# A tanh recurrence in 64 parallel chunks before a quantised FFN: warm-up steps replaced by guess steps among the x products and by corrected first steps

## The chip, the cores and the metric

One core of a Trainium2 chip. The metric is the device time of one execution in microseconds; lower is better.

## The reference

x is (2, 2048, 512) in float32, the start state (2, 512). The part of the reference that matters here:

```python
xW = einsum('ntd,dh->nth', x, Wx) + b
def step(prev_h, xw_t):
    next_h = tanh(xw_t + prev_h @ Wh)
    return next_h, next_h
_, hs = scan(step, h0, swapaxes(xW, 0, 1))       # 2048 steps, one after the other
h = relu(quant_linear(hs, w1, b1))                # 512 -> 2048
out = x + quant_linear(h, w2, b2)                 # 2048 -> 512
```

quant_linear quantises its input to 0..255 with one scale from the maximum over the whole tensor, its weights to -128..127 with one scale per row, and its bias by the product of the scales. So the first scale needs every state, and the second every hidden value.

## The kernel before, in words

**Chunks.** The 2048 steps of both sequences are cut into 64 chunks of STEPS = 32. All run at once: a state is a tile of 512 features (KT = 4 tiles of 128 partitions) by COLS = 128 columns (64 chunks x 2 sequences, chunk by chunk). Each chunk needs the last state of the chunk before it. That state is found by a warm-up: WARM = 36 steps over the columns 0 to 125 (SEAM = 126), each column running through the chunk ahead of the one whose start it gives. The recurrence forgets its start, so that warm-up and true state meet.

**Stages on PE** (`block.tensor`):
1. x products (`xw_group`, L459): 8 groups of 512 tokens, per group 4 output tiles of 4 float32 matmuls (two records each in the trace). ACT evacuates each tile with the bias to `xw` (L731). w1 and w2 land beside them and DVE makes integers of them (`integers`, L912 to L934). After each of the first three groups 16 transposes (L445) turn four blocks of w1, and ACT stores them.
2. Warm-up: three opening steps and 18 coarse guess steps with Wh and state in float16 (`products`, L484 and L491, with the x product added by a matmul with a scaled identity, L501), then 14 split steps of 48 float16 matmuls (`split_step`, L527): high and low part of Wh and of the state.
3. Main pass (`main_pass`, L484 and L491): 32 steps of 16 float32 matmuls. DVE adds the x product into the bank (`add_xw`, L953), ACT writes tanh of it as the next state (`exact_step`, L767), DVE takes each state's maximum (L1022). Inside a step, k = 0 and 1 of all four output tiles come first, then k = 2 and 3 tile by tile, so that the first tile's add and tanh run behind the others' matmuls.
4. Check of the seams (`check_seams`): DVE takes the largest difference between each chunk's last state and the start state used for the next chunk, PE turns and spreads it with the maximum (L563, L568). If it is above SEAM_TOL = 2^-17, every engine enters the repair loop (`while_seams_differ`), which puts the last states in as start states and runs the main pass again. Meanwhile PE turns 16 more weight blocks (`turn_middle`) and ACT stores them.
5. First FFN product of 8 groups (L639) with maxima over it, a short stage for the second scale (with idle products, L429), then the second FFN product (L679) with stores.

**What orders the work.** Nothing is scheduled by a program: each engine's instructions run as written, with counting semaphores. `state_ready` counts tanh tiles, `z_ready` PE's finished sums, `sum_ready` DVE's adds, `xw_free` evacuated x tiles, `w_stored` stored weight blocks.

**Where things lie.** One large SBUF tile, `arena`, holds nearly everything, and PSUM is the tensor `bank` of 8 banks; in the trace most operations are `bank<-arena` or `arena<-bank`, so lines tell them apart.

The order inside a main step on PE:

```python
for k in range(2):
    pe.wait_ge(state_ready, (n - 1) * KT + k + 1)
    for j in range(KT):
        matmul(bank[:, par * KT + j, lo:hi], weights[:, k, j * P:(j + 1) * P], source(k), ...)
for j in range(KT):
    for k in range(2, KT):
        ...
    mm.then_inc(z_ready, 1)
```

## Time and profile before

| | |
|---|---|
| Time, median of 3 runs | 540.9 us (539.24 to 541.88) |
| Span of the profiled execution | 538.5 us |
| Busy, share of the span | PE 98%, PE weight loads 62%, DVE 64%, ACT 47%, POOL 10% |
| Moved by DMA | 61.13 MB |

The span goes from the first to the last instruction of one execution on the profiler; its own time as a run is not among the three, which lie 0.7 to 3.4 us above the span. A line such as L459 is a line of the kernel before. A record's duration holds the time until its result is written, so neighbouring matmuls overlap in the view and the spacing of their starts is what a queue of them costs.

### The profile page before, as it was taken

The numbers are of one execution on the slowest core, as the hardware profiler recorded it, in microseconds if no ns is written. First come the engines' busy times: TensorE is split into PE (matmuls) and PEld (weight loads), VectorE is DVE, ScalarE is ACT, GpSimd is POOL, SyncE is SP. The second block draws the span as 40 slices with busy tenths as digits, with TensorE's granted clock in tenths as the row PEclk, the third lists the DMA queues.
The fourth block names the chain that finished last, engine by engine and source line by source line (L and its number), as shares of the span: only waits on it lengthen the run. The fifth ranks groups of instructions, "written<-read, shape, count | busy, mean of one in ns | idle before, by whom it ended". The sixth has DMA issues, their size and how long they took to land.

```text
span 538.5 us, 11182 instructions
## 1 busy us (share of the span) xinstructions
PE 525.4 (98%) x3527; PEld 332.4 (62%) x3546; DVE 342.4 (64%) x695; ACT 251.3 (47%) x558; POOL 56.0 (10%) x42
## 2 busy tenths in 40 slices
PE   7999999999999999999999899999999899999997
PEld 2444444449999999999999544444444444444443
DVE  0888880004377654555455798888868667778875
ACT  1323222226655432233223755655553866666662
POOL 2000000000000000000000000000000315354445
PEclk9999999999999999999999999999999899999999
DMA  8986500000000000000000077710000248888884
GB/s 289 323 326 252 220 1 0 0 1 1 0 0 0 2 0 0 0 0 0 0 0 0 4 292 302 301 41 0 1 1 2 78 147 311 282 318 283 319 299 145
DMA packets 21138, 61.13 MB, mean 114 GB/s; under 512 B 2032, under 2 KB 2176, under 8 KB 17536
## 3 DMA queue, kind: packets, MB, share of 16 engines
q1 hardware_dynamic: 20448, 59.84, 30.4%
q10 hardware_dynamic: 576, 1.05, 0.5%
q8 instruction: 9, 0.15, 0.1%
q0 software_dynamic: 96, 0.01, 0.1%
q14 instruction: 9, 0.07, 0.0%
HBM read 39.93 MB, written 20.97 MB: 113 GB/s over the span
## 4 chain that ended last, share of the span: by engine, by line
PE 94%; DVE 1%; DMA 1%; ACT 1%; issue 1%; DVEq 0%; ACTq 0%
PE bank L639 20%; PE bank L459 20%; PE bank L679 20%; PE bank L491 12%; PE bank L484 12%; PE bank L527 7%; DMA arena<-x_t 1%; PE bank L501 1%; PE bank L445 1%; PE bank L429 1%; ACT w1t L749 0%; DVE arena L1188 0%; ACT w2t L752 0%; DVE acc_max L1148 0%; DVE arena L1208 0%
## 5 line engine op out<-in xcount | busy, mean ns | idle before, releaser
L767 ACT ACTIVATE arena<-bank 128x126 f16<-128x126 f32 (+3 forms) x324 | 72.8, 281 | 104.1 <-DVE bank L953 74.7
L459 PE MATMUL bank<-arena 128*128 128x512 f32 (+1 forms) x256 | 111.8, 597 | 1.7 <-DMA arena<-x_t 1.7
L639 PE MATMUL bank<-arena,w1t 128*128 128x512 bf16 (+1 forms) x502 | 110.2, 379 | 2.1 <-DVE arena L1117 1.6
L679 PE MATMUL bank<-arena,w2t 128*128 128x512 bf16 x504 | 111.0, 379 | 0.6 <-DVE arena L1212 0.2
L414 POOL TENSOR_SCALAR arena<-arena,bq 128x512 f32<-128x512 f32 x32 | 52.7, 1661 | 470.0 <-DVEq L1233 415.1
L639 PEld LDWEIGHTS bank<-arena,w1t 128*128 128x128 bf16 x512 | 49.9, 98 | 62.2 <-issue 1.6
L679 PEld LDWEIGHTS bank<-arena,w2t 128*128 128x128 bf16 x512 | 49.1, 98 | 62.6 <-DVE arena L1212 4.5
L459 PEld LDWEIGHTS bank<-arena 128*128 128x128 f32 x256 | 48.5, 191 | 62.8 <-issue 61.8
L1148 DVE TENSOR_REDUCE acc_max<-arena 128x2 f32<-128x1024 f32 x60 | 71.6, 1217 | 15.8 <-ACT arena L844 15.2
L491 PE MATMUL bank<-arena 128*128 (+2 forms) x680 | 75.5, 261 | 0.5 <-ACT arena L742 0.5
L844 ACT COPY arena<-bank 128x1024 f32<-128x1024 f32 x56 | 56.7, 1012 | 40.4 <-PE bank L639 40.4
L484 PE MATMUL bank<-arena 128*128 (+2 forms) x680 | 75.1, 261 | 0.0
L868 ACT ACTIVATE arena<-arena,bias,scale 128x512 uint16 (+1 forms) x93 | 69.9, 807 | 10.5 <-DVE arena L1200 10.0
L953 DVE TENSOR_TENSOR bank<-bank,arena 128x128 f32<-128x128 f32 x128 | 38.4, 300 | 56.0 <-PE bank L491 42.3
L491 PEld LDWEIGHTS bank<-arena 128*128 128x128 f32 (+1 forms) x680 | 70.0, 169 | 0.8 <-ACT arena L742 0.7
L484 PEld LDWEIGHTS bank<-arena 128*128 128x128 f32 (+1 forms) x680 | 69.6, 169 | 0.6 <-issue 0.6
L731 ACT ACTIVATE arena<-bank,b_sb 128x512 f32<-128x512 f32 (+1 forms) x32 | 22.0, 687 | 80.5 <-PE bank L459 80.4
L1200 DVE TENSOR_SCALAR arena<-arena 128x512 bf16<-128x512 uint16 x96 | 33.2, 359 | 21.4 <-PE bank L679 18.5
L982 DVE TENSOR_SCALAR arena<-arena 128x504 f16 (+1 forms) x21 | 8.8, 422 | 55.1 <-ACT arena L731 41.0
L527 PE MATMUL bank<-arena 128*128 128x126 f16 x672 | 37.2, 218 | 0.0
L527 PEld LDWEIGHTS bank<-arena 128*128 128x128 f16 x672 | 37.0, 98 | 0.3 <-ACT arena L767 0.2
L912 DVE TENSOR_REDUCE w_absmax<-arena 128x2048 f32 x8 | 18.3, 2286 | 15.8 <-DMA arena<-w 11.8
(87 smaller groups left out, 260.6 us busy)
## 6 DMA issues: line engine op xcount, KB each, us to landing
spill<-arena SPq DMA_DIRECT2D x12, 1024.0 KB, 3.9
arena<-spill SPq DMA_DIRECT2D x12, 1024.0 KB, 8.4
arena<-w SPq DMA_DIRECT2D x8, 1024.0 KB, 5.9
arena<-x_t SPq DMA_DIRECT2D x32, 256.0 KB, 4.0
y_t<-arena SPq DMA_DIRECT2D x32, 256.0 KB, 2.1
arena<-x_t SPq DMA_DIRECT2D x7, 1024.0 KB, 8.2
arena<-x_t ACTq DMA_DIRECT2D x4, 256.0 KB, 6.2
arena<-wx SPq DMA_DIRECT2D x4, 256.0 KB, 5.5
```

The source lines that it names most:

```text
L414: nc.gpsimd.tensor_scalar(xb[:, d], xb[:, d], bq2[:, d:d + 1], None, ALU.add).then_inc(xb_ready, 1)
L459: mm = nc.tensor.matmul(bank[:, j, :], wx_sb[:, k, j * P:(j + 1) * P], x_in[:, g, k, :], start=(k == 0), stop=(k == KT - 1))
L484: nc.tensor.matmul(bank[:, par * KT + j, lo:hi], weights[:, k, j * P:(j + 1) * P], source(k), start=(first and k == 0), stop=False)
L491: mm = nc.tensor.matmul(bank[:, par * KT + j, lo:hi], weights[:, k, j * P:(j + 1) * P], source(k), start=False, stop=(k == KT - 1 and then ...
L527: return nc.tensor.matmul(bank[:, par * KT + j, 0:SEAM], weights[:, k, j * P:(j + 1) * P], state[:, 1 - par, k, 0:SEAM], **ends)
L639: mm = nc.tensor.matmul(bank[:, f % 8, :], w1t[:, k, f * P:(f + 1) * P], q[:, slot, k, :], start=(k == 0), stop=(k == KT - 1))
L679: return nc.tensor.matmul(bank[:, 4 + d, :], w2t[:, f, d * P:(d + 1) * P], hq[:, f % HQ_RING, :], start=(f == 0), stop=(f == FT - 1))
L767: return nc.scalar.activation(dst, bank[:, par * KT + j, lo:hi], ACT.Tanh, scale=scale)
L844: nc.scalar.copy(keep[:, at, f:f + 2, :], bank[:, f % 8:f % 8 + 2, :]).then_inc(acc_kept, 1)
L868: nc.scalar.activation(u[:, f % U_RING, :], src, ACT.Relu, bias=bias1[:, f:f + 1], scale=scale1[:, f:f + 1]).then_inc(u_ready, 1)
L953: nc.vector.tensor_tensor(z, z, xw[:, slot, j, 0:cols], ALU.add).then_inc(sum_ready, 1)
L1148: nc.vector.tensor_reduce(acc_max[:, g, f:f + 2], source, AX_X, ALU.max).then_inc(seen, 1)
```

## The change

The warm-up stage is gone. In its place:

- **Guess steps among the x products** (`guess_step`). Groups of x are computed in the order 3, 4, 5, 6, 7, 0, 1, 2 (X_ORDER), in 32 units of one output tile (four matmuls). From unit 13 on, the guess step for slot 13 to 31 of the chunk is put between k = 1 and k = 2 of the unit with the same number: 16 float16 matmuls with 126 columns. The first guess is tanh of slot 12's x product. ACT writes 256 times the x product into the bank before (`lay_guess`), and PE adds onto it; four matmuls with zeros (`bits_set`) make the banks add. The last guess step gives the start states of the main pass, after 19 steps.
- **Main pass** as before, but from less exact start states; in the first 12 steps DVE writes the sum before tanh to `fixed` in SBUF instead of back to the bank.
- **Correction** (`fix_step`, `fix_tanh`, `lay_fixed`, `fixes`). Twelve more steps after it: the error of a slot (new state less old, float16) times Wh in float16 is added to the saved sum before tanh, which gives the new state of the next slot, whose error goes into the next step. Slots 13 to 32 keep their states. The repair flag is raised if the last error is above 2^-17, or the first one times 2^-11 is, or Wh is too large for float16.
- The first x group now goes k by k through all four banks. The three lots of w1 transposes stand behind units 4, 7 and 10. DVE makes the float16 Wh after the fourth integer block, in two passes instead of four, with a maximum of Wh. Tokens are numbered on by `tokens(g)`, so that the corrected groups are quantised from `fixed`.

```diff
-PRE = 4
-WARM = PRE + STEPS
-COARSE = 22
+GUESS = 20
+FIXED = 12
+LEFT_OUT = 2.0 ** -11
+FIRST_GROUP = (STEPS - GUESS) // SLOTS_PER_GROUP
+X_ORDER = tuple((i + FIRST_GROUP) % GROUPS for i in range(GROUPS))
+TURN_BEHIND = {4: 0, 7: 1, 10: 2}
-MIDDLE_BANKS = (2, 3, 4, 5, 6, 7)
+MIDDLE_BANKS = (4, 5, 6, 7, 2, 3)
...
+            def guess_step(s):
+                n = s - (STEPS - GUESS)
+                pe.wait_ge(guess_laid, n)
+                for j in range(KT):
+                    for k in range(KT):
+                        if j == 0 and k % 2 == 0:
+                            pe.wait_ge(guess_ready, 2 * (n - 1) + k // 2 + 1)
+                        mm = nc.tensor.matmul(guess_bank(s, j), wh_high[:, k, j * P:(j + 1) * P],
+                                              guess[:, (n - 1) % 2, k, 0:SEAM], start=False,
+                                              stop=(k == KT - 1), skip_group_check=True)
+                    if j % 2 == 1:
+                        mm.then_inc(guess_z, 1)
...
+            def fix_step(t):
+                at, par = 4 * (t % 2), (t - 1) % 2
...
+                pe.wait_ge(fixed_laid, t)
+                pe.wait_ge(error_ready, 2 * t - 1)
+                for j, k in ((0, 0), (1, 0), (0, 1), (1, 1), (2, 0), (3, 0)):
+                    add(j, k)
+                pe.wait_ge(error_ready, 2 * t)
+                for j, k in ((0, 2), (0, 3), (1, 2), (1, 3)):
+                    mm = add(j, k)
+                mm.then_inc(fixed_z, 1)
+                for j, k in ((2, 1), (2, 2), (2, 3), (3, 1), (3, 2), (3, 3)):
+                    mm = add(j, k)
+                mm.then_inc(fixed_z, 1)
...
+                    for k in range(KT):
+                        mm = x_product(i, j, k)
...
+                        if k == 1 and unit > STEPS - GUESS:
+                            if unit == STEPS - GUESS + 1:
+                                pe.wait_ge(wh_split, 1)
+                            guess_step(unit)
...
-            first_guess_step()
...
-            with pe.Fori(COARSE // 2, WARM // 2) as half:
-                split_step(half * 2, 0)
-                split_step(half * 2 + 1, 1)
             pe.wait_ge(wh_in, 16)
             pe.wait_ge(h0_in, 16)
-            main_pass(WARM)
+            pe.wait_ge(xw_free, KT + GROUPS * KT)
+            main_pass(0)
+            for t in range(1, FIXED + 1):
+                fix_step(t)
...
+            def fix_tanh(t):
+                at = 4 * (t % 2)
+                for a in range(2):
+                    act.wait_ge(fixed_z, 2 * (t - 1) + a + 1)
+                    nc.scalar.activation(fixed[:, t - 1, 2 * a:2 * a + 2, :],
+                                         bank[:, at + 2 * a:at + 2 * a + 2, 0:COLS], ACT.Tanh,
+                                         scale=1.0 / WH_SCALE).then_inc(fixed_ready, 1)
...
+            for t in range(1, FIXED + 1):
+                fix_tanh(t)
+                if t + 2 <= FIXED:
+                    lay_fixed(t + 2)
...
+            def fix_pair(t, a):
+                dve.wait_ge(fixed_ready, 2 * (t - 1) + a + 1)
+                nc.vector.tensor_tensor(error[:, t % 2, 2 * a:2 * a + 2, 0:SEAM],
+                                        fixed[:, t - 1, 2 * a:2 * a + 2, BATCH:COLS],
+                                        states[:, t, 2 * a:2 * a + 2, BATCH:COLS],
+                                        ALU.subtract).then_inc(error_ready, 1)
```

How the change moves the instructions, at three places. First PE, at the end of the x products (L459 before). Before, the loop over the last four groups was followed by the opening of the warm-up (L484 and L491 with Wh, L501 with the identity):

```order
L473 COMPARE_AND_BRANCH
L484 MATMUL bank<-arena 128x124 x8
L491 MATMUL bank<-arena 128x124 x2
L501 MATMUL bank<-arena,idf 128x124
L491 MATMUL bank<-arena 128x124 x2
L501 MATMUL bank<-arena,idf 128x124
```

Now (L468 an x product, L553 the zeros, L483 a guess step) the x products go on in fours with a guess step between each two fours:

```order
L464 MATMUL bank<-id,w1t 128x128 x16
L468 MATMUL bank<-arena 128x512 x6
L553 MATMUL bank<-arena 128x256 x4
L468 MATMUL bank<-arena 128x512 x4
L483 MATMUL bank<-arena 128x126 x16
L468 MATMUL bank<-arena 128x512 x4
L483 MATMUL bank<-arena 128x126 x16
```

Each four are the second half of one unit and the first half of the next; the last guess step is followed by two x products and then by the main loop.

Second, PE at the end of the main pass. Before, its loop was followed at once by the turning of weights (L445) and the spreading of the maximum (L563, L568):

```order
L553 COMPARE_AND_BRANCH
L445 MATMUL bank<-id,w1t 128x128 x16
L445 MATMUL bank<-id,w2t 128x128 x28
L563 MATMUL bank<-id,stat 1x128 x2
L445 MATMUL bank<-id,w2t 128x128 x8
```

Now 192 matmuls, 16 for each correction step, stand between the loop and the same row:

```order
L505 COMPARE_AND_BRANCH
L515 MATMUL bank<-arena 128x126 x192
L464 MATMUL bank<-id,w1t 128x128 x16
L464 MATMUL bank<-id,w2t 128x128 x28
L574 MATMUL bank<-id,stat 1x128 x2
L464 MATMUL bank<-id,w2t 128x128 x8
```

Third, ACT at the same place. Before, the loop over the main steps (L767) was followed by the stores of turned weights:

```order
L767 ACTIVATE arena<-bank 128x128
L809 REGISTER_ALU
L809 COMPARE_AND_BRANCH
L749 COPY w1t<-bank 128x4x128 x4
L752 COPY w2t<-bank 128x512 x12
```

Now the last two main steps (L797) are written out, with the laying of saved sums (L817) between them, and then each correction step's two tanh (L824) are followed by the laying for the step after the next:

```order
L797 ACTIVATE arena<-bank 128x128 x4
L817 ACTIVATE bank<-arena 128x4x128
L797 ACTIVATE arena<-bank 128x128 x4
L817 ACTIVATE bank<-arena 128x4x128
L824 ACTIVATE arena<-bank 128x256 x2
L817 ACTIVATE bank<-arena 128x4x128
L824 ACTIVATE arena<-bank 128x256 x2
```

The pattern goes on to the twelfth step; the stores of turned weights come after it.

## Rows read from the trace of the kernel before

**Rows 1.** The page: PE's busy time (part 1) and granted clock by slice (part 2).
```profile
PE 525.4 (98%) x3527; PEld 332.4 (62%) x3546; DVE 342.4 (64%) x695; ACT 251.3 (47%) x558; POOL 56.0 (10%) x42
...
PEclk9999999999999999999999999999999899999999
```

**Rows 2.** Busy time by stage: split steps, main steps, the stage behind them.
```profile
core 0: us, PE busy (x) PEld busy (x) DVE busy (x) ACT busy (x) POOL busy (x), PEclk, DMA share, GB/s
...
146.00:183.00 37.00, 37.00 (x672) 36.93 (x673) 28.02 (x111) 20.71 (x113) 0.00 (x0) 1.00 0.00 0
183.00:297.40 114.40, 114.40 (x1028) 114.40 (x1026) 58.50 (x160) 35.48 (x129) 0.00 (x0) 1.00 0.00 0
297.40:305.40 8.00, 5.84 (x70) 4.20 (x71) 5.95 (x20) 7.67 (x18) 0.00 (x0) 1.00 0.01 2
```

**Rows 3.** Order of time on PE, x products: start, us, instruction [idle before it].
```profile
5.03 2.75 PE L459 MATMUL bank<-arena 128*128 128x512 f32 x4 [0.35 <-DMA arena<-x_t]
9.14 12.26 PE L459 MATMUL bank<-arena 128*128 128x512 f32 x28 [1.36 <-DMA arena<-x_t]
...
22.12 13.95 PE L459 MATMUL bank<-arena 128*128 128x512 f32 x32
35.91 1.06 PE L445 MATMUL bank<-id,w1t 128*128 128x128 bf16 x16
...
51.49 68.89 PE L459 MATMUL bank<-arena 128*128 128x512 f32 x160
120.21 0.60 PE L484 MATMUL bank<-arena 128*128 128x124 f16 x8
```

**Rows 4.** Order of time: a weight load of PE, and DVE's integer blocks.
```profile
6.34 0.61 PEld L459 LDWEIGHTS bank<-arena 128*128 128x128 f32 x2 [0.84 <-DMA arena<-wx]
...
12.91 2.29 DVE L912 TENSOR_REDUCE w_absmax<-arena 128x2048 f32 x1 [11.77 <-DMA arena<-w]
...
18.93 1.23 DVE L934 TENSOR_SCALAR w1t<-arena 128x2048 f32 x1 [0.15 <-DVE arena L924]
...
42.28 1.23 DVE L934 TENSOR_SCALAR w1t<-arena 128x2048 f32 x1 [0.15 <-DVE arena L924]
```

**Rows 5.** Order of time on PE: the split steps and the first main matmuls.
```profile
145.94 37.25 PE L527 MATMUL bank<-arena 128*128 128x126 f16 x672
183.02 2.02 PE L484 MATMUL bank<-arena 128*128 x16
```

**Rows 6.** Groups by line and shape: busy us, mean ns of one, idle before.
```profile
L953 DVE TENSOR_TENSOR bank<-bank,arena 128x128 f32<-128x128 f32 x128 | 38.4, 300 | 56.0 <-PE bank L491 42.3
L527 PE MATMUL bank<-arena 128*128 128x126 f16 x672 | 37.2, 218 | 0.0
...
L767 ACT ACTIVATE arena<-bank 128x128 f32 x128 | 35.5, 277 | 79.1 <-DVE bank L953 74.7
...
L1022 DVE TENSOR_REDUCE slot_max<-arena x32 | 21.9, 686 | 0.0
...
L1034 DVE TENSOR_TENSOR arena<-arena 128x378 f32<-128x378 f32 x1 | 0.5, 543 | 0.0
```

**Rows 7.** Order of time: handovers at the warm-up's start and in a main step.
```profile
120.41 0.69 ACT L731 ACTIVATE arena<-bank,b_sb 128x512 f32<-128x512 f32 x1 [2.55 <-PE bank L459]
...
121.35 0.42 PE L491 MATMUL bank<-arena 128*128 128x124 f16 x2 [0.54 <-ACT arena L742]
...
185.63 1.64 DVE L953 TENSOR_TENSOR bank<-bank,arena 128x128 f32<-128x128 f32 x4 [2.11 <-PE bank L491]
186.08 0.69 ACT L767 ACTIVATE arena<-bank 128x128 f32 x2 [2.26 <-DVE bank L953]
```

**Rows 8.** Busy time by stage, two us each, before the second FFN product.
```profile
415.00:417.00 2.00, 1.30 (x10) 0.48 (x7) 1.50 (x2) 1.01 (x1) 0.00 (x0) 1.00 0.00 0
417.00:419.00 2.00, 0.68 (x9) 0.32 (x7) 1.43 (x6) 1.50 (x2) 0.00 (x0) 1.00 0.91 260
...
421.00:423.00 2.00, 2.00 (x6) 0.68 (x5) 1.02 (x5) 2.00 (x4) 0.00 (x0) 0.50 0.00 0
```

More of the change, by code:

```diff
@@ L95 @@
 STAT_LINKS = 6
+STAT_FIRST = 4
 def rnn_ffn_program(nc, xT, h0T, wx, wh, bT, w1, b1T, w2, b2T, ident, yT):
@@ L481, in products @@
+            def products(n, at, state):
                 for k in range(2):
-                    pe.wait_ge(state_ready, (n - 1) * KT + k + 1)
+                    pe.wait_ge(state_ready, n * KT + k + 1)
                     for j in range(KT):
-                        nc.tensor.matmul(bank[:, par * KT + j, lo:hi],
-                                         weights[:, k, j * P:(j + 1) * P], source(k),
-                                         start=(first and k == 0), stop=False)
+                        nc.tensor.matmul(bank[:, at + j, 0:COLS], wh_sb[:, k, j * P:(j + 1) * P],
+                                         state(k), start=(k == 0), stop=False)
@@ L489, in products @@
                         if j == 0:
-                            pe.wait_ge(state_ready, (n - 1) * KT + k + 1)
-                        mm = nc.tensor.matmul(bank[:, par * KT + j, lo:hi],
-                                              weights[:, k, j * P:(j + 1) * P], source(k),
-                                              start=False,
-                                              stop=(k == KT - 1 and then_add is None))
-                    if then_add is not None:
-                        mm = then_add(j)
@@ L550, in split_step @@
+                            pe.wait_ge(state_ready, n * KT + k + 1)
+                        mm = nc.tensor.matmul(bank[:, at + j, 0:COLS],
+                                              wh_sb[:, k, j * P:(j + 1) * P], state(k),
+                                              start=False, stop=(k == KT - 1))
                     mm.then_inc(z_ready, 1)
@@ L797, in _, with guess_pair @@
[L797 to L809 removed]
+            def guess_pair(s, a):
+                at = 4 + 2 * (s % 2) + a
+                return bank[:, at, 0:2 * COLS].rearrange("p (k c) -> p k c", k=2)[:, :, 0:SEAM]
@@ L820, in repair @@
             def repair(r):
-                main_pass(WARM + r * STEPS)
+                early_steps(r * STEPS)
+                with act.Fori(FIXED // 2, STEPS // 2) as half:
+                    for par in range(2):
+                        late_step(r * STEPS, half * 2 + par, par)
                 act.wait_ge(flag_ready, r + 1)
```

484 lines of the change are left out of this document (245 added, 239 removed).

## The prediction

> **What bounds the kernel now.** I read the page's shares and slices first: PE is busy 98% of a 538.5 us span, at the full clock but for one slice [rows 1]. The sum is made against that span; the three timed runs have their median, 540.9 us, 2.4 us above it, and I carry the difference in us over to the median. A high PE share does not say that every matmul is limited by the array, so the second view was busy time by stage [rows 2]: in the split warm-up PE is busy 37.00 of 37.00 us, in the main steps 114.40 of 114.40, and only in the eight microseconds after them do holes appear (5.84 of 8.00). DVE and ACT have slack in each of these stages. So until 297.4 us the time is the number of matmuls times the spacing at which PE starts them, and a change there is worth what it takes off PE's queue, if the other engines still keep up. The third view, PE's order of time, gives the spacings [rows 3, 5].
>
> **What is removed.** The whole warm-up goes: from the first guess matmul at 120.21 us [rows 3] to the first main matmul at 183.02 us [rows 5], **62.8 us**. Of this the 14 split steps are 37.1 us (672 matmuls), the 21 coarse ones the rest. POOL's copy of the identity goes too, beside other work, and so does DVE's second half of the split of Wh: it ran while PE worked on x products, so it is worth nothing.
>
> **What is added between the x products.** 19 guess steps of 16 matmuls, 128x126 f16. The row of the same form gives 672 starts in 37.25 us, whose last record alone lasts 0.218 [rows 5, 6]: (37.25 - 0.16) / 672 = 55.2 ns. So 304 x 55.2 ns = **+16.8 us**, all on PE's path, since PE has no idle time there. A change from x products to 128-column matmuls and back costs something: 32 records between two lots of transposes take 35.91 - 22.12 = 13.79 us, while the last 160 take 120.21 - 51.49 = 68.72, or 13.74 per 32 [rows 3]. That is 0.05 us a time, 19 times: **+1.0**. Four idle matmuls of 256 columns: **+0.4** (twice 55 ns each).
> The Trainium skill, TensorE: Matmul & The Clock Gate, section Back-to-back issue gap, speaks against this part: pairs of weight load and matmul sustain about 81 ns at 128 columns. By that figure the 304 would be an estimated 24.6 us instead of 16.8; the trace disagrees, its 672 such pairs stand at 55 ns.
>
> Is a guess step ever late? A unit of x products (four matmuls, eight records) is 3.4 us, with the guess step in its middle 4.3 us. From one step's sums to the next step ACT must do two tanh of 2x126 columns, lay x products of a later step into a bank (504 columns) and evacuate 512: about 0.4 + 0.4 + 0.7 + 0.7 = 2.2 us, the last from the 0.69 of such an evacuation [rows 7]. It fits twice into 4.3, and the tanh comes first. So no PE wait is charged. DVE now splits Wh after the fourth integer block, which ends at 43.5 us [rows 4]; two passes of the size of 1.23 end by about 46, and the first guess step comes at about 54. The four w2 blocks are then some 5 us later, with 60 us of x products over them.
>
> **The opening.** Before, bank 0 took all its four k before bank 1 began, so PE sat until x's later quarters landed at 9.14, with four records done since 5.03 [rows 3]. Now all four banks take k=0, then k=1. k=1's weights are there at 6.34 [rows 4], and 16 records at 0.43 us (68.72 / 160) reach from 5.03 to 11.9, past 9.14. 32 records end at 5.03 + 13.75 = 18.8 instead of 21.2: **-2.4 us**. The next unit needs the second group of x, queued right behind the first w block, which landed at 12.91 [rows 4]; its 1 MB should follow in some 3 us, before 18.8. The transposes now stand one unit later, at about 22.2, and their integers are ready at 20.16 [rows 4]. If the DMA comes later the gain is nil: bounds 0 and -2.5.
>
> **A new stop before the main steps.** They wait for the last evacuation of x. PE's last x record ended at 120.38, and ACT evacuated from 120.41 for 0.69, to 121.10 (PE's next start that needed ACT, 121.35, came after a tanh more) [rows 7]. With a handover of 0.06, between the two named below, PE could go on at 121.16; without the wait it would at 120.21. **+0.95**. The main steps themselves stay 32 x 16 matmuls with add and tanh behind them. The first 12 write their sums to SBUF instead of PSUM; ACT starts 0.15 us after DVE's end (185.63 + 0.30, then 186.08) [rows 6, 7] and both idle over a microsecond per step, so nothing is charged.
>
> **The correction steps.** Twelve steps that nothing covers: PE, ACT and DVE wait for each other in a ring. The engines' queues per step: PE 16 matmuls, ACT two tanh of 256 columns and one laying of 512, DVE two differences of 252 and a maximum over 512. Prices: tanh 256 lies between 277 ns (128 columns) [rows 6] and 0.69 us (512) [rows 7], by columns 0.41; a difference of 252 lies between 300 ns (128) and 543 (378) [rows 6], 0.42. The ring through the second half: ten matmuls till its sums are there, 9 x 0.055 + 0.218 = 0.71; tanh 0.41; difference 0.42; three handovers, of which rows show 0.03 (PE to ACT, 120.38 to 120.41) and 0.15 (DVE to ACT) [rows 7], say 0.2 together: **1.75 us a step**. ACT's own work, 0.41 + 0.41 + 0.69 = 1.5, and DVE's, 0.42 + 0.42 + 0.69 = 1.5, fit below it, though not by much. Lower bound 1.5 (those queues, no handovers), upper 2.2 (0.15 for each handover, and the laying or the maximum in the way of the next tanh or difference).
> Lead-in after the last main matmul: add 0.30 and tanh 0.28 with handovers, 0.9; DVE has the maximum of step 31 (686 ns [rows 6]) in front of the first difference; two differences; 1.8 us. Then 11 rings and the last ten-odd matmuls, 0.78: 1.8 + 19.3 + 0.8 = **+21.8 us**.
>
> **Behind it** stand the 16 transposes and their stores, the seam's maximum, the scale and the quantising, as before. The seam's chain loses one difference and the add, and has more in one piece; PE was waiting for ACT's stores as much as for it. Taken as **-0.3**, bounds -1 and +1. The FFN stages keep their matmuls; the order of token groups and the one new wait of ACT (for DVE's third quantising, which DVE does before the first maxima) are costed at nothing: DVE runs two groups ahead of PE there.
>
> Sum: -62.8 + 16.8 + 1.0 + 0.4 - 2.4 + 0.95 + 21.8 - 0.3 = -24.5 us. Span 538.5 - 24.5 = 514.0; **time 540.9 - 24.5 = 516.4 us**. With the bounds (ring 1.6 to 1.95, opening, tail) this case reaches from 513 to 520.5.
>
> **The rivals.**
> Long rings (14%). Handovers sit three times in each step, and ACT's laying comes right before the next tanh. At 2.25 us a step the stage is 12 x 0.5 = 6 us longer: 522.4. Against it: the queues sum to 1.5 us only.
> The clock falls (13%). In the correction steps PE streams 16 x 0.055 = 0.88 us of each 1.75, about half. For it: before the FFN's second half, PE was busy 1.30 and then 0.68 of 2 us, and by 421 us the granted clock was 0.50, the 1.2 GHz level [rows 8]. Against it: through the 8 us after the main steps, where some 68 matmuls of 128 columns stream 3.8 us (47%), it stayed at 1.00 [rows 2], and half is nearer to that. At 1.2 GHz 128 columns take 0.107 us instead of 0.053, ten in a row 0.5 more: 12 x 0.55 = 6.6, and about 1.5 more until the first FFN products have it back: 524.5.
> The Trainium skill, TensorE: Matmul & The Clock Gate, section A second HAM failure mode: psum-queue depth-cycling, states this rule: frequent short idling of PE between groups of matmuls makes the clock swing between its levels. By it the result is that of this rival.
> The repair loop runs (4%): the one that ends slower. The flag is raised when a difference left after 12 corrected steps is above 2^-17 = 7.6e-6, or the first one times 2^-11 is. Carrying out the new arithmetic on the reference's inputs, with float16 where the kernel has it, I get 0.0010 for the first difference (0.06 of its limit) and 4.9e-6 for the last (0.64 of it), shrinking by some 0.64 a step. It decides from a start error 1.6 times as large. Then a main pass of 114.4 us is run again [rows 2], with a seam check of about 8 and a copy of some 4: 516.4 + 126 = 643 us.
> The interleaving isn't free (3%): if PE's queue loses 0.4 us at each of 19 steps, by late tanh or late weights, 7.6 us: 524.
>
> **Chances.** The sum as it stands has 66%; 516.4 is its value. All cases but the repair loop are faster by far more than 0.5% (2.7 us, about what a measurement of this kernel can tell from no change): faster 0.95, same 0.01 for something unseen that eats all of it, slower 0.04. The range takes in the forecast's own and three of the rivals, 511.5 to 525 us.
>
> **What the profile would show.** Right: no hole in PE from 5 us to the end of the x products, at about 136.0 us; the first record of the main steps about 0.9 us after that; 12 groups of correction matmuls 1.7 to 1.9 us apart with PE idle less than a microsecond in each; the first FFN product near 281 us; PEclk 9 in all slices but one. Wrong: idle time of the guess matmuls "from ACT" (the interleaving), correction tanh ending over 2 us apart (the ring), a PEclk digit below 9 near 260 us (the clock), or more than 512 main products (the repair).

## The result, and the profile after

| | before | after |
|---|---|---|
| Time, median of 4 runs each | 540.71 us | **517.88 us** (517.40 to 518.74) |
| Ratio, 95% interval | | 0.9585 (0.9568 to 0.9602) |
| Span of the profiled execution | 538.5 us | 515.9 us (its run: 517.75 us) |

The change takes 22.6 us off the span, where the sum said 24.5. The page after, busy time and granted clock by slice, beside [rows 1]:

```profile
PE 496.1 (96%) x2954; PEld 300.8 (58%) x2954; DVE 310.6 (60%) x587; ACT 256.5 (50%) x455; POOL 55.8 (11%) x41
...
PE   8999999999999999999857999999998999999997
...
PEclk9999999999999999999999999999998999999999
```

PE runs 573 matmul records fewer (3527 in [rows 1]). The slices "857" are the correction steps and what follows them, the new stretch in which PE waits for the other engines. Stage by stage, PE's order of time (start, us, instruction, idle before it), beside [rows 3, 5]:

```profile
4.87 18.47 PE L468 MATMUL bank<-arena 128*128 128x512 f32 x40 [0.20 <-DMA arena<-wx]
23.18 1.06 PE L464 MATMUL bank<-id,w1t 128*128 128x128 bf16 x16
...
55.65 1.04 PE L483 MATMUL bank<-arena 128*128 128x126 f16 x16
56.53 3.65 PE L468 MATMUL bank<-arena 128*128 128x512 f32 x8
60.02 1.04 PE L483 MATMUL bank<-arena 128*128 128x126 f16 x16
...
135.19 1.94 PE L468 MATMUL bank<-arena 128*128 128x512 f32 x4
138.33 2.05 PE L493 MATMUL bank<-arena 128*128 x16 [1.21 <-ACT arena L729]
...
255.48 1.04 PE L515 MATMUL bank<-arena 128*128 128x126 f16 x16 [1.50 <-ACT bank L817]
257.21 1.04 PE L515 MATMUL bank<-arena 128*128 128x126 f16 x16 [0.69 <-DVE arena L1037]
259.06 1.04 PE L515 MATMUL bank<-arena 128*128 128x126 f16 x16 [0.81 <-DVE arena L1037]
...
275.51 1.06 PE L464 MATMUL bank<-id,w1t 128*128 128x128 bf16 x16
...
282.64 7.54 PE L637 MATMUL bank<-arena,w1t 128*128 128x512 bf16 x33 [1.21 <-DVE arena L1167]
```

The last x record ends at 135.19 + 1.94 = 137.13 and lasts 0.60 (the others of the group are done before), so it starts at 136.53, and the x products leave PE's queue one spacing of 0.43 later, at 136.96. Put against the sum, stage by stage:

| stage | forecast, us | measured, us |
|---|---|---|
| end of x products (before 120.21) | +15.8 (16.8 + 1.0 + 0.4 - 2.4) | +16.75 |
| stop before the main steps | 0.95 | 1.37 (136.96 to 138.33) |
| main steps, 114.4 before | 114.4 | 115.48 (138.33 to 253.81) |
| correction steps | 21.8 | 21.70 (253.81 to 275.51) |
| from there to the first FFN product, 7.97 before | 7.67 | 7.13 |
| the rest | +0 | +0.17 |

The x products, the stop and the main steps miss upward by 0.95 + 0.4 + 1.1, some 2.5 us; the tail and the correction steps give 0.6 back, the rest takes 0.2, and some 2 us remain, 24.5 against 22.6. The experiments take the larger ones one by one.

### The profile page after: what moved, and what is told of

It reads as the page before. It is cut to its first block, busy times and chain, and to the rows that moved or that the text cites. A ratio compares the mean times of both kernels' runs of the same rounds, so it can differ in the third digit from the quotient of the medians.

```text
span 515.9 us, 9080 instructions
## 1 busy us (share of the span) xinstructions
PE 496.1 (96%) x2954; PEld 300.8 (58%) x2954; DVE 310.6 (60%) x587; ACT 256.5 (50%) x455; POOL 55.8 (11%) x41
## 3 DMA queue, kind: packets, MB, share of 16 engines
q10 hardware_dynamic: 576, 1.05, 0.6%
## 4 chain that ended last, share of the span: by engine, by line
PE 93%; DVE 3%; ACT 2%; issue 1%; DVEq 0%
PE bank L468 22%; PE bank L637 22%; PE bank L677 21%; PE bank L493 11%; PE bank L499 11%; PE bank L483 3%; PE bank L515 2%; PE bank L448 1%; DVE arena L1037 1%; PE bank L464 1%; ACT arena L824 1%; ACT w1t L737 0%; DVE arena L1238 0%; DVE arena L1262 0%; DVE acc_max L1198 0%
## 5 line engine op out<-in xcount | busy, mean ns | idle before, releaser
L468 PE MATMUL bank<-arena 128*128 128x512 f32 x256 | 116.2, 602 | 0.2 <-DMA arena<-wx 0.2
L1198 DVE TENSOR_REDUCE acc_max<-arena 128x2 f32<-128x1024 f32 x60 | 71.6, 1217 | 15.8 <-ACT arena L875 15.2
L468 PEld LDWEIGHTS bank<-arena 128*128 128x128 f32 x256 | 47.3, 192 | 51.4 <-issue 50.3
L994 DVE TENSOR_TENSOR arena<-bank,arena 128x128 f32 x48 | 14.0, 292 | 91.5 <-PE bank L499 91.2
L493 PE MATMUL bank<-arena 128*128 x512 | 63.5, 277 | 1.2 <-ACT arena L729 1.2
L499 PE MATMUL bank<-arena 128*128 x512 | 62.4, 275 | 0.0
L493 PEld LDWEIGHTS bank<-arena 128*128 128x128 f32 x512 | 59.7, 192 | 2.2 <-issue 2.0
L499 PEld LDWEIGHTS bank<-arena 128*128 128x128 f32 x512 | 59.7, 192 | 0.0
L797 ACT ACTIVATE arena<-bank 128x128 f32 (+1 forms) x80 | 22.2, 277 | 48.6 <-DVE bank L1001 46.1
L1001 DVE TENSOR_TENSOR bank<-bank,arena 128x128 f32<-128x128 f32 x80 | 24.0, 300 | 36.5 <-PE bank L499 27.6
L1250 DVE TENSOR_SCALAR arena<-arena 128x512 bf16<-128x512 uint16 x96 | 31.4, 340 | 20.7 <-PE bank L677 17.7
L729 ACT ACTIVATE arena<-bank,b_sb 128x512 f32<-128x512 f32 x32 | 21.7, 687 | 34.9 <-PE bank L468 34.9
L797 ACT ACTIVATE arena<-arena x48 | 14.8, 309 | 30.7 <-DVE arena L994 26.6
L762 ACT ACTIVATE arena<-bank 128x252 f16<-128x252 f32 x36 | 13.7, 380 | 27.5 <-PE bank L483 26.4
```

The costliest lines, as they stand in the source:

```text
L468: return nc.tensor.matmul(bank[:, j, :], wx_sb[:, k, j * P:(j + 1) * P], x_in[:, X_ORDER[i], k, :], start=(k == 0), stop=(k == KT - 1))
L493: nc.tensor.matmul(bank[:, at + j, 0:COLS], wh_sb[:, k, j * P:(j + 1) * P], state(k), start=(k == 0), stop=False)
L499: mm = nc.tensor.matmul(bank[:, at + j, 0:COLS], wh_sb[:, k, j * P:(j + 1) * P], state(k), start=False, stop=(k == KT - 1))
L797: nc.scalar.activation(dst(j), src(j), ACT.Tanh).then_inc(state_ready, 1)
L1001: nc.vector.tensor_tensor(z, z, xw[:, s, j, :], ALU.add).then_inc(sum_ready, 1)
L1198: nc.vector.tensor_reduce(acc_max[:, g, f:f + 2], source, AX_X, ALU.max).then_inc(seen, 1)
```

## The experiments

### The stop before the main steps

PE's chain there, from the chain of waits (start, us, what):

```profile
137.16 0.70 ACT arena L729
137.86 0.47 issue
```

The wait ends with ACT's evacuation at 137.86, and then 0.47 us pass in which nothing is shown before the loop's first matmul. The forecast had 0.06 for this handover. The experiment puts the wait into the loop, where it is needed first (the second step uses the banks of the last x unit):

```diff
...
                     for par in range(2):
+                        if par == 1:
+                            pe.wait_ge(xw_free, KT + GROUPS * KT)
                         products(first + s + par, 4 - 4 * par, ...)
...
-            pe.wait_ge(xw_free, KT + GROUPS * KT)
+            pe.wait_ge(state_ready, KT)
             main_pass(0)
```

> The wait for the last evacuation of x stands before the second main step (whose banks it guards) instead of before the first; before the first stands only the wait for the four start-state tiles. In the trace of the changed kernel PE stood 1.42 us between the x products and the main steps, of which 0.69 are the evacuation and 0.48 its handover to PE. Theory A (the stop is nothing but that wait): the main steps begin within 0.1 us of the last x product's slot, time 517.9 - 1.4 = 516.5 us. Theory B (entering the loop on PE costs its 0.5 us whatever it waits for): 0.9 us off, about 517.0. Theory C (the evacuation is late for the second step as well): unchanged.

Measured: 516.66 us (514.96 to 516.93), 0.9554 (0.9535 to 0.9572), 1.2 us under the changed kernel's 517.88. PE no longer stops:

```profile
134.63 1.94 PE L468 MATMUL bank<-arena 128*128 128x512 f32 x4
136.40 1.95 PE L493 MATMUL bank<-arena 128*128 x16
...
253.43 1.04 PE L517 MATMUL bank<-arena 128*128 128x126 f16 x16 [1.50 <-ACT bank L819]
255.16 1.84 PE L517 MATMUL bank<-arena 128*128 128x126 f16 x16 [0.69 <-DVE arena L1039]
257.39 1.58 PE L517 MATMUL bank<-arena 128*128 128x126 f16 x16 [0.39 <-DVE arena L1039]
259.62 1.04 PE L517 MATMUL bank<-arena 128*128 128x126 f16 x16 [0.65 <-DVE arena L1039]
```

The last x record leaves the queue at 134.63 + 1.94 - 0.60 + 0.43 = 136.40, and the main steps start at 136.40. So the whole stop of 1.37 us is avoidable, its 0.47 us too: the loop is entered before anything is waited for. The first correction matmul comes 2.05 us earlier (253.43 instead of 255.48), of which 0.56 are not the edit's: in this execution the x products were that much earlier (134.63 instead of 135.19), for a reason given under the opening. And the span fell by only 1.0, since time is lost again behind that: the second and third group of correction matmuls take 1.84 and 1.58 instead of 1.04. The windows of two stretches (PE, PEld, DVE, ACT, POOL busy, then granted clock):

```profile
255.00:257.00 2.00, 1.84 (x16) 1.61 (x16) 1.71 (x5) 0.91 (x2) 0.00 (x0) 0.54 0.05 8
259.00:261.00 2.00, 1.04 (x16) 0.90 (x16) 1.61 (x4) 1.63 (x5) 0.00 (x0) 1.00 0.00 0
```

The granted clock is 0.54 here (0.61 in the two microseconds that follow), at its 1.2 GHz level for most of this stretch, and back at 1.00 by 259 us, in the middle of the same rings. This is the rival of the falling clock, but with two rings of 2.23 us instead of 1.85 and 1.73, so 0.9 us where it had 8.

### The slower first main steps

PE's main steps are 3.57 us apart from the fourteenth on, as before, but the first 13 are 3.66 us apart. The order of time in one that writes its sums to SBUF: the add of its first tile, the four tanh, and PE's next step in its two halves (k = 0 and 1, then k = 2 and 3); then the first half of the fourteenth step:

```profile
148.35 0.29 DVE L994 TENSOR_TENSOR arena<-bank,arena 128x128 f32 x1 [2.02 <-PE bank L499]
...
148.88 1.57 ACT L797 ACTIVATE arena<-arena  x4 [2.08 <-DVE arena L994]
149.35 2.04 PE L493 MATMUL bank<-arena 128*128 x16
151.22 1.95 PE L499 MATMUL bank<-arena 128*128 x16
...
185.91 1.95 PE L493 MATMUL bank<-arena 128*128 x16
```

and the group of these tanh over the whole run (busy us, mean ns of one, idle before):

```profile
L797 ACT ACTIVATE arena<-arena x48 | 14.8, 309 | 30.7 <-DVE arena L994 26.6
```

The tanh takes 309 ns from SBUF against 277 from PSUM [rows 6], and it starts 0.24 us after the add's end (148.35 + 0.29, then 148.88) against 0.15 [rows 7]. That is some 0.1 us for each tile, and it counts for one tile only, the first. Its tanh ends at 148.88 + 0.31 = 149.19, just ahead of the next step's first matmul at 149.35, and the half that begins there takes 2.04 (to its last result) where the fourteenth step's takes 1.95: that is the 0.09 by which the step is longer. The last tile's tanh ends at 148.88 + 1.57 = 150.45, and the half that reads it starts at 151.22 without a hole. Twelve steps write to SBUF and hold back the twelve steps behind them; the first step is long as well (3.70), and stays so with the sums in PSUM (3.67 in the run that follows), so that is not theirs. The experiment leaves the sum in PSUM, lets ACT read it there as before, and copies four sums at once behind the step's tanh:

```diff
-                        exact_tanh(first + s + par, lambda j: fixed[:, s + par, j, :],
+                        exact_tanh(first + s + par, lambda j: bank[:, 4 - 4 * par + j, 0:COLS],
...
+                    z = bank[:, at + j, 0:COLS]
...
-                    nc.vector.tensor_tensor(fixed[:, s, j, :], bank[:, at + j, 0:COLS], xw[:, s, j, :],
-                                            ALU.add).then_inc(sum_ready, 1)
+                    nc.vector.tensor_tensor(z, z, xw[:, s, j, :], ALU.add).then_inc(sum_ready, 1)
+                dve.wait_ge(state_ready, (n + 1) * KT + KT)
+                nc.vector.tensor_copy(fixed[:, s], bank[:, at:at + KT, 0:COLS]).then_inc(sum_kept, 1)
```

> In the first 12 main steps DVE adds into the bank, as in the others, ACT reads the bank, and DVE copies the four sums to SBUF afterwards, outside the chain. In the changed kernel these steps took 3.66 us each instead of 3.57. Theory A (the sum's way over SBUF makes the next step's first matmul late: handover 0.24 instead of 0.15, tanh 309 instead of 277 ns): back to 3.57, 1.0 us less, 516.9. Theory B (something else at the start of the main steps, such as the approximate start states or DVE's loop without the maximum): stays at 3.66, unchanged or more, since DVE has the copies too.

Measured: 517.34 us (516.17 to 518.78), 0.9575 (0.9555 to 0.9596). In the trace, against the same rows of the changed kernel (138.33 and 255.48, 117.15 apart), main start and first correction matmul are 116.11 apart:

```profile
137.59 2.05 PE L494 MATMUL bank<-arena 128*128 x16 [1.21 <-ACT arena L730]
...
253.70 1.04 PE L516 MATMUL bank<-arena 128*128 128x126 f16 x16 [1.50 <-ACT bank L818]
```

The 1.04 us, twelve times 0.09, are there in the trace. The times alone, 0.5 us apart with overlapping intervals, would not show it.

### The opening

The first x group goes bank by bank again:

```diff
...
-                    for to in range(KT):
-                        pe.wait_ge(xw_free, to + 1)
-                        mm = x_product(0, to, j)
...
+                    for k in range(KT):
+                        if j == 0:
+                            pe.wait_ge(wx_in[k], 16)
+                            pe.wait_ge(x0_in[k], 16)
+                        mm = x_product(0, j, k)
...
```

> Only the opening undone: the first x group goes bank by bank again, so PE waits in bank 0 for the later quarters of x. The prediction put the opening at 2.4 us; by the trace of the changed kernel it brought about 1.5, since PE's first records there stand 0.86 us apart instead of 0.43. Theory A (those first records are slow whatever follows, and the waits of before hid that): 1.5 us more, 519.4. Theory B (prediction): 2.4 more, 520.3.

Measured: 519.83 us (518.46 to 520.65), 0.9619 (0.96 to 0.9639): the median is 1.95 us above the changed kernel's, between the two theories' 1.5 and 2.4. PE's order of time:

```profile
8.55 15.93 PE L468 MATMUL bank<-arena 128*128 128x512 f32 x36 [1.22 <-DMA arena<-x_t]
24.31 1.06 PE L464 MATMUL bank<-id,w1t 128*128 128x128 bf16 x16
```

40 records are done at 24.31 against 23.18: 1.13 us between these two executions. Before, the fifth record began at 9.14 [rows 3], so 40 would have been done at 9.14 + 36 x 0.4295 = 24.6, and the change gained 1.4 against that. The 2.4 us of the forecast are not reached in this execution because the first records are slow. PE's weight loads in the changed kernel, each ahead of its record:

```profile
5.85 0.34 PEld L468 LDWEIGHTS bank<-arena 128*128 128x128 f32 x1 [0.52 <-issue]
6.71 0.34 PEld L468 LDWEIGHTS bank<-arena 128*128 128x128 f32 x1 [0.52 <-issue]
7.30 0.19 PEld L468 LDWEIGHTS bank<-arena 128*128 128x128 f32 x1 [0.25 <-issue]
```

They stand 0.86 us apart, then 0.59, and 0.43 from there on. The 40 records take 18.31 us where 40 x 0.4295 is 17.18. So 1.13 us go to the first records, which run at half the rate, as at the 1.2 GHz level. The windows of 4.8 to 7.3 us read a granted clock of 1.00 all the same, but the trace's first record of the clock begins at 7.02 us in this execution, so nothing stands under that figure.

How many records are slow differs from execution to execution. In the profile of a kernel that opens in the same way (the one with filled holes, below) all but the first stand 0.43 apart:

```profile
4.84 17.41 PE L468 MATMUL bank<-arena 128*128 128x512 f32 x40 [0.17 <-issue]
```

Over the twelve profiles of kernels with the new order the 40 records are done between 21.88 and 23.25 us, at 22.8 on average, and in each the full rate comes with the first record of the clock, from 4.38 to 7.37 us. With the old order PE waits for x in any case: 24.31 here, 24.6 before. So the order is worth 1.1 to 2.7 us, some 1.7 on average, and the forecast's 2.4 where the clock is up early. The same spread, 1.4 us, moves everything behind the opening, and it is why the experiments are compared by distances within a trace.

### What sets the ring

The changed kernel's first ring, from 255.48 on PE to 257.21; the order of time on ACT and DVE in it:

```profile
256.22 0.71 ACT L824 ACTIVATE arena<-bank 128x256 f32<-128x256 f32 x2 [0.86 <-PE bank L515]
...
256.64 0.75 DVE L1037 TENSOR_TENSOR arena<-arena 128x252 f16<-128x252 f32 x2
```

Ten matmuls to their sums 0.74; tanh 0.38; 0.04 to DVE; difference 0.42; 0.15 to PE: 1.73 us through the first half, where the forecast had 0.71 + 0.41 + 0.42 + 0.2 = 1.74. It had named this the ring through the second half; whether the two halves differ, the first of three experiments asks, by four matmuls in the first group instead of six, so that the first half's sums come two matmuls earlier (the two go to the last group):

```diff
-                for j, k in ((0, 0), (1, 0), (0, 1), (1, 1), (2, 0), (3, 0)):
+                for j, k in ((0, 0), (1, 0), (0, 1), (1, 1)):
...
```

> In each correction step PE issues four matmuls before it waits for the second difference instead of six, so the first sums are complete after 8 matmuls instead of 10. Theory A (the ring runs through the first half: ten matmuls, first tanh, first difference): each ring 0.11 us shorter, 1.73 to about 1.62, time 1.2 us less, 516.7. Theory B (the second difference, which ends some 0.18 us after a ring's first matmul, is then what the ring runs through): 1.73 to 1.68, 0.6 us less. If DVE's or ACT's queue set the pace: no change.

Measured: 518.23 us (516.69 to 519.03), 0.9587 (0.9568 to 0.9607). From the fourth ring on they are not shorter but longer, 1.77 us. The second group:

```profile
257.08 1.18 PE L515 MATMUL bank<-arena 128*128 128x126 f16 x16 [0.58 <-DVE arena L1037]
```

The group takes 1.18 instead of 1.04, so PE now stands inside it: the second difference comes about 0.33 us after the first, just what six matmuls take (6 x 0.055). With four ahead PE waits for it, and then twelve matmuls, not ten, lead to the second half's sums. Without those two the ring through the second half would be some 0.1 us shorter, an estimated 1.66, so the two halves lie within a tenth of a microsecond of each other, and neither theory came true.

Is DVE's queue in the way? Here the maxima over the corrected slots 1 to 11 are left out (one small copy, once, stands for them):

```diff
-                    nc.vector.tensor_reduce(slot_max[:, t:t + 1], fixed[:, t - 1, :, :], AX_XY, ALU.max)
...
+                        nc.vector.tensor_copy(slot_max[:, 1:FIXED], slot_max[:, FIXED + 1:2 * FIXED])
```

> Leaves out DVE's maxima of 512 columns over the corrected slots 1 to 11, so the input's scale lacks them. Theory A (the ring is 10 matmuls, tanh, difference and handovers; DVE has 0.4 us to spare per step): rings stay at 1.73 us, only the second one, which held two maxima, falls from 1.85 to 1.73; time 0.1 us less. Theory B (DVE's queue sets the pace): rings 0.3 or more shorter, 3 to 4 us less.

Measured: 518.09 us (one run). The rings stay at 1.73. Only the second one, 1.85 in the changed kernel where two maxima stand in it, becomes 1.73 too:

```profile
257.25 1.04 PE L515 MATMUL bank<-arena 128*128 128x126 f16 x16 [0.69 <-DVE arena L1037]
258.98 1.04 PE L515 MATMUL bank<-arena 128*128 128x126 f16 x16 [0.69 <-DVE arena L1037]
```

Is ACT's? The laying of a saved sum is done twice, and in a further kernel four times:

```diff
+                for i in range(2 - 1):
+                    nc.scalar.activation(bank[:, at:at + KT, 0:COLS], fixed[:, t - 1], ACT.Identity,
+                                         scale=WH_SCALE).then_inc(lay_link, 1)
+                    act.wait_ge(lay_link, (2 - 1) * (t - 1) + i + 1)
```

> ACT lays each saved sum twice, one after the other, so 0.6 us and a short wait more per correction step in ACT's queue. Theory A (ACT has 0.5 us between the end of a laying and the next tanh): rings longer by 0.2 us only, time 2 us more. Theory B (the ring is ACT's queue): 0.7 us a ring, 7 to 8 us more.

> The same with four layings: rings of about 3.5 us, in which PE has 0.88 us of matmuls, a quarter instead of half. This tests the rival on the clock. Theory A (clock held at half, but not at a quarter, as in the stage before the second FFN product): the granted clock falls to 0.50 within the correction steps, matmuls start every 0.107 us there, and time is 18 us more for ACT's queue plus 2 us or so until the FFN has the clock back. Theory B (the clock holds also at a quarter): 1.00 throughout, 18 us more.

Measured: 516.98 us with two (one run), rings of 1.84; 533.43 us with four (one run), rings of 3.105. The first time is below the changed kernel's although its rings are longer, by 1.05 us from the first correction matmul to the last: its mean granted clock is 1.00, so the clock never fell, and it says nothing on the layings. Twice, order of time on PE; four times, on ACT and on PE:

```profile
258.70 1.04 PE L516 MATMUL bank<-arena 128*128 128x126 f16 x16 [0.86 <-DVE arena L1042]
260.54 1.04 PE L516 MATMUL bank<-arena 128*128 128x126 f16 x16 [0.80 <-DVE arena L1042]
```

```profile
257.81 1.87 ACT L819 ACTIVATE bank<-arena 128x512 f32<-128x512 f32 x3
259.71 0.60 ACT L822 ACTIVATE bank<-arena 128x512 f32<-128x512 f32 x1
260.25 0.64 ACT L829 ACTIVATE arena<-bank 128x256 f32<-128x256 f32 x2
```

```profile
261.21 1.84 PE L516 MATMUL bank<-arena 128*128 128x126 f16 x16 [2.06 <-DVE arena L1042]
```

ACT's starts say what its queue costs: 260.92 - 260.25 = 0.67 for the two tanh, 1.90 / 3 = 0.63 for a laying ahead of another one, 0.54 for the last (259.71 to 260.25). That makes 0.67 + 0.63 + 0.54 = 1.84 with two layings and 0.67 + 1.90 + 0.54 = 3.11 with four, which are the rings measured, and 0.67 + 0.54 = 1.21 in the changed kernel: 0.5 us of slack in 1.73. So the ring is set by the latencies through PE, ACT and DVE, and by no engine's queue, except with the layings added. The long-rings rival is out. What was expected of the longer queues was too high, since durations were added where starts count.

With four layings the clock falls and stays down through this stage, as theory A had it: granted 0.63 from 259 to 262 us, 0.50 from there to 290, PE's groups of 1.84 instead of 1.04. The 533.43 us hold hardly any of that, since ACT's queue covers it.

### How far the repair loop is

Two kernels tighten the bound, by 0.6 and by 0.2, and change nothing else:

```diff
-SEAM_TOL = 2.0 ** -17
+SEAM_TOL = 0.6 * 2.0 ** -17
```

> The same kernel with the seam tolerance at 0.6 of its value. The arithmetic worked through for the prediction gave 0.64 of the limit for the last difference, so the flag should be raised once: a second main pass with its check, priced at 126 us: about 644 us. If the chip's difference is smaller than that arithmetic's, no repair and 517.9.

> The seam tolerance at 0.2 of its value, since 0.6 raised no flag. Theory A (the chip's last difference is near the arithmetic worked through for the prediction, if below 0.6 of the limit): the flag is raised and one repair runs, priced at 126 us (a main pass of 114.4, a seam check, a copy): about 644 us. Theory B (the chip's differences are much smaller than worked out): 517.9.

Measured: 517.39 us with 0.6 (one run), no repair; the last difference on the chip is below 0.6 of the bound, where I had worked out 0.64. With 0.2: **730.45 us** (one run), one repair. That is 212.6 us more than the changed kernel, where the rival had 126. The order of time on DVE and PE, and the window behind the second main pass:

```profile
481.29 0.88 DVE L1157 TENSOR_SCALAR arena<-arena,s_in_inv 128x512 uint16<-128x512 f32 x2 [71.06 <-issue]
495.36 19.82 PE L637 MATMUL bank<-arena,w1t 128*128 128x512 bf16 x81 [85.52 <-issue]
```

```profile
410.00:495.00 85.00, 0.00 (x0) 0.05 (x2) 7.42 (x20) 0.00 (x0) 0.00 (x0) 0.50 0.00 0
```

The pass, the copy (3.35 us) and the seam check are about the 126 us: they end at 410 us, where the changed kernel's first FFN product starts at 282.6. Then, with the seams in order, PE does nothing for 85.5 us. The repair loop is a fixed loop of 63 rounds (CHUNKS - 1) with a flag tested in each; one round repairs and 62 load the flag and branch. Each engine walks through them by itself: PE takes 85.5 / 62 = 1.38 us for a round, DVE 71.06 / 62 = 1.15, so DVE quantises from 481.29 on while PE is still in its rounds, and PE ends last. The trace also records what the engines' sequencers do: a round of PE holds one flag load of 0.30 us and two branches of 0.21, a round of DVE the same load and two branches of 0.06, so neither the load nor the branches alone are the round.

### The clock

How often does it fall in the changed kernel? The mean granted clock of each execution tells it: in the profiles, one short fall goes with 0.996 or 0.997, two with 0.993, and none with 1.00. Before the change, of 21 executions 4 had 0.994, 3 had 0.999 or 1.00, and 14 had 0.996 or 0.997, as the profiled one with its fall at [rows 8]. With the correction steps 0.993 comes in more than half of them: 2 of 4 of the changed kernel (518.00 and 518.74 us against 517.75 and 517.40), 4 of 5 with the wait moved, 2 of 5 with four matmuls first, 3 of 5 with the sums in PSUM (one of them at 0.987) and with the opening undone. PE is busy for 12.47 of the 21.70 us of the correction stage:

```profile
253.80:275.50 21.70, 12.47 (x194) 10.76 (x193) 17.87 (x41) 15.17 (x37) 0.00 (x0) 1.00 0.01 2
```

If those holes were the cause, filling them should cure it. Useless matmuls of 256 columns, twelve before and four behind each correction step, into unused columns:

```diff
...
+                if t < FIXED:
+                    pe.wait_ge(fixed_laid, t + 1)
+                    fill(4, 4 * ((t + 1) % 2))
...
             main_pass(0)
+            pe.wait_ge(fixed_laid, 1)
+            fill(12, 4)
```

> Matmuls without use fill PE's holes in the correction stage: 12 of 256 columns (1.3 us) before its first step, 4 (0.43 us) after each step, into columns nobody reads, of the four banks that ACT is not using. Nothing else changes. Theory A (in about half of the executions the granted clock falls to 0.50 for a short stretch in the correction steps, as in the profile of the run with the wait moved, because of the holes there; those are the executions with a mean clock of 0.993 instead of 0.996 or 0.997): no execution at 0.993, the stage's rings stay 1.73 us, and the median comes down by some 0.6 to 1 us to about 517.1. Theory B (the lower mean clock comes from elsewhere, or useless matmuls delay the ring): executions at 0.993 remain, or the rings get longer than 1.75 and the time rises.

Measured: 517.68 us (517.31 to 518.24), 0.9578 (0.9561 to 0.9594). The fill costs nothing, rings stay 1.73, PE is busy for 18.59 us of a stage as long as before, and 3 of 5 executions still have 0.993. In its profile the correction stage stays at 1.00 and the second fall lies elsewhere, at the first FFN products behind the turning of weights:

```profile
280.00:282.00 2.00, 0.34 (x4) 0.30 (x6) 1.74 (x7) 2.00 (x5) 0.00 (x0) 0.83 0.02 4
282.00:284.00 2.00, 1.91 (x5) 0.76 (x5) 1.96 (x7) 0.83 (x2) 0.00 (x0) 0.50 0.03 8
```

So a fall can come in either place. In the correction stage only the profiles with the moved wait and with four layings have one; between 279 and 285 us, behind the turning of weights, six have one: this one, four matmuls first, the two with a tighter bound, and the two with both repairs. Four matmuls first and the bound at 0.6 have no other, so a mean of 0.996 or 0.997 does not say that the fall lies where it lay before. The theory that the holes between the correction groups alone bring the second fall is refuted. Why two falls come more often than before stays open; the stage behind the correction steps, at whose end most of them lie, was not changed in any run.

A fall costs what PE loses in it: 0.9 us in the rings above, where other engines set the pace for half of the time. Between executions of one kernel the price comes out at 0.4 us (with the fill) to 1.9 us (both repairs and the fill, next section).

### Both repairs together

The moved wait and the sums in PSUM, with no other edit; and the same with the fill:

> The moved wait and the sums in the bank together: main steps begin with the last x product's end and take 3.57 us each. By the traces -1.3 and -1.0 us: 515.5 us. If the two pay for the same wait: no less than the better of them alone, 516.6.

> The same two and the filled holes. If the fill keeps the clock: 514.7 us and no execution at a mean clock of 0.993. If the fill costs more than the clock: above the run without it.

Measured: **514.49 us** (513.33 to 516.14), 0.9522 (0.9501 to 0.9543); with the fill 514.76 us (512.29 to 517.09), 0.9521 (0.949 to 0.9552). The first in its order of time:

```profile
136.56 1.95 PE L494 MATMUL bank<-arena 128*128 x16
...
252.58 1.04 PE L518 MATMUL bank<-arena 128*128 128x126 f16 x16 [1.50 <-ACT bank L820]
...
280.13 10.19 PE L640 MATMUL bank<-arena,w1t 128*128 128x512 bf16 x40 [1.59 <-DVE arena L1172]
```

The main steps follow the x products at once, and from their start to the first correction matmul it is 116.02 us against 117.15: the two gains, 1.37 and 1.13, add up. The first FFN product starts 2.51 us earlier than in the changed kernel (282.64); that this is just their sum is chance, since an opening 0.4 us earlier and a second fall around 280 us take each other away. The median lies 3.4 us lower, 0.9 more than the trace shows, with executions 2.8 us apart. The kernel beats both others. The fill brings nothing that the intervals show: its six executions are 512.29 to 513.27 us where the mean clock is 0.999 or 1.00, and 516.25 to 517.09 where it is 0.993, 3.8 us for two falls.

## Why the prediction was right

516.4 us against 517.88, inside the range. Each step by what it measured:

- **Warm-up gone, guess steps between the x products: right.** A unit with its guess step takes 60.02 - 55.65 = 4.37 us, which is 8 x 0.4295 + 16 x 0.0552 + 0.05. No hole appears in any of the 19. The Trainium skill, TensorE: Matmul & The Clock Gate, section Back-to-back issue gap, has about 81 ns for a pair of weight load and matmul at 128 columns; the trace does not agree, with 56.53 - 55.65 = 0.88 us for 16 of them, 55 ns each.
- **The opening: mis-sized.** "2.4 us" was 1.4 in the profiled execution; undoing the order cost 1.13 in the trace. The step that failed is "16 records at 0.43 us reach from 5.03 to 11.9": the first ones stand 0.86 apart, until the clock is up. Where it is up early (40 records done at 21.88 and 22.08) the gain is the forecast's or a little more.
- **The stop: right in kind, mis-sized,** 0.95 for 1.37. The handover of 0.06 was chosen between two that the rows show, 0.03 from PE to ACT and 0.15 from DVE to ACT, and neither leads to PE; ahead of the loop it is 0.47.
- **The main steps: "nothing is charged" was wrong,** 1.08 us. The reason given, that both engines idle over a microsecond per step, doesn't bear on it: the first tile's add and tanh are on the path from one step to the next, since PE's next step begins with that tile. Before, its tanh ended 0.30 us ahead of the next step's first matmul (186.08 + 0.28 [rows 6, 7], then 186.66 below), and in the changed kernel 0.16 ahead, with that matmul held; of the 0.1 us added there PE could absorb next to nothing. The other three tiles have time, and ACT's idle time lies before the first sum, where it can't be used. Putting the sums back into PSUM gave 1.04 of it back. The row is of the kernel before, order of time on PE:

```profile
186.66 1.50 PE L484 MATMUL bank<-arena 128*128 x12
```

- **The correction steps: right,** 21.70 for 21.8, by 1.67 lead-in, rings of 1.73 (the second 1.85) and the last group. The tanh of 256 columns took 0.38 and the difference 0.42, for 0.41 and 0.42. It was named as the ring through the second half and is the one through the first; that both come to nearly the same sum is luck.
- **The tail:** -0.84 for -0.3, within the bounds of -1 and +1. No run says where the other 0.5 come from, and they hide as much of the misses above.
- **The falling clock: half right.** It was priced as a stage at the lower level, 8 us; it comes as one short fall more, in somewhat more than half of the executions, for 0.4 to 1.9 us, and mostly behind the correction steps. Its for and against also set unlike figures beside each other, PE's streamed time (0.88 of 1.75) and its busy time (1.30 and 0.68 of 2). The Trainium skill, TensorE: Matmul & The Clock Gate, section A second HAM failure mode: psum-queue depth-cycling, has short idling between groups of matmuls make the clock swing. The swing at 255 us with the moved wait agrees (0.54, 0.61, then 1.00 again); the rest of the same rings at 1.00 doesn't, and neither do the second falls that stayed with the fill (3 of 5 executions), though these lay outside the filled stage in the one profile.
- **The repair loop** didn't run, as weighed. Its price lacked the empty rounds: 212.6 us for 126.

## What to carry to other kernels

Whether an edit beside the bound engine is free depends on whether that engine waits for its result next, and not on how idle its own engine is: a result moved from PSUM to SBUF cost 0.09 us a step, by the one tile of four with which the next step begins. A wait for buffers belongs ahead of the first instruction that writes them, and not ahead of the loop: that alone was worth 1.4 us in the trace. A short dependent ring is priced well as a sum of latencies, but an engine's queue by the distance of its starts; and a loop that hardly ever runs should be priced with all of its empty rounds. Gains of a microsecond are read from distances within a trace, since the start of the clock alone moves the rest of this kernel by up to 1.4 us.

## What was not expected of the hardware

- PE's first float32 records run at half rate, 0.86 us apart against 0.43, up to a time that differs by execution (4.38 to 7.37 us). The view's granted clock of 1.00 before it has no record of the clock under it.
- ACT starts an operation up to 0.1 us before the one ahead of it ends: two tanh of 0.38 us take 0.67, and a laying of 0.60 takes 0.54 ahead of a tanh, but 0.63 ahead of a laying that waits for its end.
- A handover from DVE to ACT takes 0.15 us with the sum in PSUM and 0.24 with it in SBUF, and the tanh of 128 columns 277 and 309 ns.
- PE's first matmul of a loop came 0.47 us after the wait ahead of the loop had ended, against 0.15 from DVE's end within the rings. That it is the loop's entry is read from the place; it wasn't tried by itself.
- A round of a loop that only loads a flag and branches takes 1.38 us on PE and 1.15 on DVE, and all through 62 of them PE's granted clock is at 0.50.
